# A merged latent entry, queries projected early, a later copy, and unread products on TensorE in the last batch and behind it

## The chip, the cores and the metric

One core of a Trainium2 chip runs the whole program in one launch. The metric is the device time in microseconds (us), the median of repeated runs. Five engines work side by side: PE (TensorE, matrix products), DVE (VectorE), ACT (ScalarE), POOL (GpSimd, which also issues the indirect DMAs, the ones that take row numbers from a tile) and SP (SyncE, which issues plain DMAs). Each engine runs its own list of instructions in order and waits on semaphores. All data are float32.

## The reference, cut to what matters

```python
# B = 16 batches of T = 112 tokens, D = 256, context of S = 375 rows, 16 heads of 64
x = x + L0_xcond(layernorm(x), cond, ctx)     # block 0: self-attention, cross-attention, gated GELU feed-forward
x = x + L0_ffn(layernorm(x))                  # 64 experts, the best 8 of each token, and a shared one
x = x + L1_xcond(ctx, layernorm(x), cond)     # latent attention: keys from layernorm(ctx) and the latents
x = x + L1_ffn(x)                             # 8 experts, the best one of each token
# in L1_xcond: lat = layer_norm(layernorm(x)) * w + b, so that the rows are normalised twice
```

## The kernel before, in words

The program has four stages, one after the other. The order on each engine is written by hand. Only semaphores tie the engines together.

**Block 0** (16 batches, the function `batch(b, begin, last)` on every engine; batches 1 to 14 are a hardware loop). PE does for a batch: scores, transposes and outputs of the self-attention; `project_out(wo1)`; values of the context; a transpose of the normalised rows (`transpose_h(hn2)`); the first half of the cross queries (`wq2`, heads 0 to 7); a transpose of the *next* batch's rows (`transpose_h(hn1)`); then `attention`, the cross-attention, in four steps k = 0, 2, 4, 6 of two head pairs each. Within a step PE makes scores (L966), DVE their negated maxima (`nmax`, L2126), ACT the exponentials (`probs`, L1678), PE transposes them (L978), DVE and ACT copy the transposes (`probsT`), and PE multiplies with the values (L991). The hook `late` puts work between the scores and the transposes of step 0: the ranks of the routing of the batch before, and the second half of the cross queries, into the PSUM bank `psO[:, 1]`. Behind the attention follow the projections of the next batch's queries and keys (`half_qk(wq1)` twice, `half_qk(wk1)` twice), and then `project_out(wo2)`, which waits for DVE's scaled outputs `oT` (L2077). Last comes the feed-forward with its 64 instructions of up projection (`fw1`) and `project_out(fw2)`. ACT computes `hT1` and `hT2` from the transposed rows (`affine`, L1709). The same DVE does the routing of the batch before in small chained pieces (`slots`, with `route_piece` between the steps), and POOL scatters the routed slots to a table in memory, each scatter behind a numbered job of DVE (`SCATTER_JOBS`).

**Experts 0.** Behind the last batch come the shared expert's products (`shared_up`, `shared_down`), the counting of the routed rows (`tables0`), a gather of the row numbers (`idrow`), a transpose of them (L1316), and then `blocks0`, which takes 144 blocks of rows: POOL gathers their rows, PE transposes them (L1405), DVE copies the transposes (`xT0`, L2582), PE multiplies (L1421, L1433), and ACT stores the results to `ydram`, in memory as `expert_rows` (L1815).

**Latent attention** (16 batches, `batchL`). Its entry: keys and values of the first context; DVE adds the eight expert rows of each token to X (`add_rows`, L2661), which POOL has gathered into `yk` by `fetch0` (L795, eight indirect DMAs); statistics; `latents0` on DVE normalises the rows of batch 0 twice in a row, with two inverse roots (`inverse_root_column`, three Newton steps each); PE transposes the latents (L1572) and projects them. Then DVE adds the expert rows of batch 1, all eight in a row, before it takes up the first attention. POOL does for each later batch `latents(b)`, `fetch0(b + 1)` and `context_rows(b + 1)`. PE's `transpose_kv(b)` needs `lat_ready`, which POOL's `latents(b)` raises. `fetch0(0)` follows a wait for all stores of experts 0.

**Experts 1** is the last stage. Its first two weights, of 2 MB each, are issued by SP (`weights1(0)`, `weights1(1)`) as soon as the last product of experts 0 is done.

## Time and profile before

| what | value |
|---|---|
| median of 3 runs | 2773.25 us (2772.94 to 2776.93) |
| the profiled execution | 2777.12 us, its span 2775.0 us |
| PE busy | 2649.2 us, 95% of the span |
| DVE busy | 1515.7 us, 55% |
| ACT busy | 1101.0 us, 40% |
| POOL busy | 903.2 us, 33% |
| mean granted clock of TensorE | 0.984 |

The span runs from the first to the last instruction. A clock of 1.00 is TensorE's full speed (2.4 GHz), 0.50 is the other level (1.2 GHz). The ends of PE's instructions are modelled, so that an idle time before a matmul is good to about a tenth of a microsecond.

### The profile page before, as it was taken

Reading aid. Unit: us, or ns where it says so; the run is one execution under the profiler, and the core shown is the slowest. Engines: PE = TensorE matmul, PEld = TensorE weight load, DVE = VectorE, ACT = ScalarE, POOL = GpSimd, SP = SyncE. Lnnn points to the kernel's source line nnn. Section 1 sums busy time; section 2 is a strip of 40 time slices with the busy share of each in tenths; the row PEclk is TensorE's granted clock in tenths of the full one; section 3 lists DMA queues with packets and bytes.
Section 4 is the critical chain, followed back from the end, with each engine's and each line's share of the span. In section 5 each row is a group of like instructions: output and inputs, shape, how many; then the busy total and the mean of one; then the engine's idle time right before and its main releaser. Section 6 shows DMA issues by size and latency. Waiting matters only on the chain. (4 is left out here: it accounts for less than half of the span.)

```text
span 2775.0 us, 61020 instructions
## 1 busy us (share of the span) xinstructions
PE 2649.2 (95%) x18023; PEld 1838.3 (66%) x18024; DVE 1515.7 (55%) x4435; ACT 1101.0 (40%) x2902; POOL 903.2 (33%) x1743
## 2 busy tenths in 40 slices
PE   8999999999999999998899988999999999999698
PEld 5777776777777767775566645665666665656597
DVE  4555555555555555555666645655556655554332
ACT  2443444334434443343366623443334433334222
POOL 2121112222211222221455526444444344440343
PEclk9999999999999999999899999999999999999799
DMA  7000000000000000002588841000010000100351
GB/s 243 4 9 7 9 9 9 9 9 3 7 7 9 9 9 9 9 4 99 173 255 254 198 127 38 26 22 22 22 39 27 22 22 22 30 18 5 99 179 26
DMA packets 87780, 145.65 MB, mean 52 GB/s; under 512 B 22418, under 2 KB 64399, under 8 KB 86176
## 3 DMA queue, kind: packets, MB, share of 16 engines
q1 hardware_dynamic: 44320, 84.85, 9.6%
q0 software_dynamic: 20848, 41.09, 5.7%
q10 hardware_dynamic: 22544, 18.89, 2.0%
q8 instruction: 33, 0.54, 0.1%
q14 instruction: 35, 0.29, 0.0%
HBM read 116.17 MB, written 29.51 MB: 53 GB/s over the span
## 5 line engine op out<-in xcount | busy, mean ns | idle before, releaser
L1037 PE MATMUL psG<-W,ctxT 128*125 128x512 f32 (+2 forms) x896 | 406.8, 597 | 4.8 <-DVE v L2754 4.8
L1031 PE MATMUL psG<-ctxT,W 128*128 128x375 f32 (+1 forms) x1024 | 385.6, 524 | 2.8 <-ACT ctxT L1910 1.5
L1031 PEld LDWEIGHTS psG<-ctxT,W 128*128 128x128 f32 x1024 | 189.3, 190 | 161.3 <-issue 106.7
L1678 ACT ACTIVATE probs<-psG,nmax 112x375 f32<-112x375 f32 (+1 forms) x384 | 233.1, 618 | 147.2 <-DVE nmax L2126 147.2
L1037 PEld LDWEIGHTS psG<-W,ctxT 128*125 128x125 f32 (+2 forms) x896 | 160.8, 187 | 180.6 <-issue 170.2
L1025 PEld LDWEIGHTS psG<-hT,W 128*128 128x128 f32 x2304 | 267.3, 194 | 17.1 <-ACT hT L1709 14.8
L1025 PE MATMUL psG<-hT,W 128*128 128x112 f32 x2304 | 272.2, 278 | 1.9 <-ACT hT L1709 1.9
L2126 DVE TENSOR_REDUCE nmax<-psG 112x1 f32<-112x375 f32 (+1 forms) x384 | 208.6, 599 | 64.3 <-PE psG L966 60.2
L664 POOL DMA_INDIRECT slot_table<-stt,st x120 | 114.1, 951 | 340.7 <-DVE qT L2155 124.3
L991 PEld LDWEIGHTS psO<-probsT,v 125*64 125x64 f32 (+2 forms) x3584 | 173.3, 137 | 65.2 <-issue 61.1
L991 PE MATMUL psO<-probsT,v 125*64 125x112 f32 (+2 forms) x3584 | 200.5, 263 | 0.0
L966 PE MATMUL psG<-kT,qT 64*112 64x375 f32 (+1 forms) x768 | 169.6, 545 | 19.1 <-ACT hT L1709 17.8
L771 POOL DMA_INDIRECT W<-normed_rows,ids x144 | 136.2, 946 | 127.8 <-PE psG L1405 101.1
L1049 PE MATMUL psG<-W,oT 128*112 128x256 f32 x768 | 173.9, 380 | 2.0 <-DVE oT L2077 2.0
L1049 PEld LDWEIGHTS psG<-W,oT 128*112 128x112 f32 x768 | 133.5, 177 | 36.0 <-issue 9.8
L978 PE MATMUL psG<-ident,probs 112*122 112x112 f32 (+1 forms) x1120 | 143.8, 267 | 2.9
L1421 PE MATMUL psG<-W 128*64 (+1 forms) x936 | 141.6, 390 | 0.2
L795 POOL DMA_INDIRECT mlp<-expert_rows,st x128 | 121.0, 945 | 47.5 <-issue 35.2
L1942 ACT ACTIVATE v<-psG 122x512 f32<-122x512 f32 x64 | 38.2, 597 | 242.6 <-PE psG L1037 242.6
L978 PEld LDWEIGHTS psG<-ident,probs 112*122 112x122 f32 (+1 forms) x1120 | 110.6, 140 | 25.3 <-ACT probs L1678 16.1
L2754 DVE COPY v<-psG 122x512 f32<-122x512 f32 x64 | 44.2, 691 | 131.9 <-PE psG L1037 131.9
L966 PEld LDWEIGHTS psG<-kT,qT 64*112 64x112 f32 x768 | 62.0, 173 | 67.7 <-ACT hT L1709 20.9
(428 smaller groups left out, 4704.3 us busy)
## 6 DMA issues: line engine op xcount, KB each, us to landing
W<-in_ew SPq DMA_DIRECT2D x64, 384.0 KB, 4.3
expert_rows<-W ACTq DMA_DIRECT2D x144, 128.0 KB
W<-in_ew SPq DMA_DIRECT2D x8, 2048.0 KB, 8.3
ctxT<-in_ctxT SPq DMA_DIRECT2D x16, 375.0 KB, 3.1
kT<-in_ctx SPq DMA_DIRECT2D x16, 375.0 KB
normed_rows<-hrow SPq DMA_DIRECT2D x32, 112.0 KB, 1.9
W<-normed_rows,ids POOLq DMA_INDIRECT x144
slot_table<-stt,st POOLq DMA_INDIRECT x136, 2.1
```

The source lines that it names most:

```text
L771: nc.gpsimd.indirect_dma_start(out=xg0[:, j % 4, :], out_offset=None, in_=hd, in_offset=bass.IndirectOffsetOnAxis(ap=ids[:, j:j + 1], axis ...
L795: nc.gpsimd.indirect_dma_start(out=yk[:, k, :], out_offset=None, in_=ydram[0], in_offset=bass.IndirectOffsetOnAxis(ap=st8[:, 0, k:k + 1], ...
L966: nc.tensor.matmul(pair_bank(order, slot, i)[0:T, 0:keys], qT[DH * i:DH * i + DH, u, :], kT[DH * i:DH * i + DH, u, 0:keys], start=True, st ...
L978: mm = nc.tensor.transpose(pair_bank(order, turned_slot(u), i)[0:ke, c * T:(c + 1) * T], probs[:, 2 * (u % 2) + i, k0:k0 + ke], ident[0:T, ...
L991: mm = nc.tensor.matmul(psO[DH * i:DH * i + DH, u // 4, (u % 4) * T:(u % 4 + 1) * T], v[0:kn, c, h * DH:(h + 1) * DH], probsT[0:kn, u % 2, ...
L1025: mm = nc.tensor.matmul(bank[:, j * T:(j + 1) * T], wt[:, c, n0 + j * P:n0 + (j + 1) * P], hT[:, c, :], start=(c == 0), stop=(c == DC - 1))
L1031: mm = nc.tensor.matmul(bank[:, 0:n], wt[:, c, n0 + j * P:n0 + (j + 1) * P], src[:, c, 0:n], start=(c == 0), stop=(c == DC - 1))
L1037: mm = nc.tensor.matmul(bank[0:kn, 0:512], src[:, c, k0:k0 + kn], wt[:, c, n0 + half * 512:n0 + (half + 1) * 512], start=(c == 0), stop=(c ...
L1049: mm = nc.tensor.matmul(bank[0:T, 0:D], oT_[:, c, :], wo[:, c, :], start=(c == 0), stop=(c == n - 1))
L1421: mm = nc.tensor.matmul(psG[half * h:half * h + half, 2 + j.m2, 0:256], xT0[:, j.m, c, half * h:half * h + half], weights(c, k, h), start= ...
L1678: nc.scalar.activation(probs[:, 2 * (u % 2) + i, 0:keys], pair_bank(order, scores_slot(u), i)[0:T, 0:keys], ACT.Exp, bias=nmax[:, h:h + 1] ...
L2126: nc.vector.tensor_reduce(nmax[:, 2 * u + i:2 * u + i + 1], pair_bank(order, scores_slot(u), i)[0:T, 0:keys], AXX, ALU.max, negate=True).t ...
```

## The change

Six edits:

- *Early queries.* In batches 0 to 14 PE projects the second half of the cross queries ahead of the attention's scores, not between scores and transposes. At that old place it now projects the first half of the next batch's keys (`next_keys`, bank `psO[:, 0]`), so that one projection less stands behind the attention. DVE copies these keys there; ACT copies the second half. DVE's routing pieces move back by one, the last three to a new place `behind` the attention, and POOL's scatters change the jobs that they wait for.
- *Later copy.* In the self-attention DVE normalises two tiles of `probs` before it copies the first transpose (`self_copy(0)`).
- *Unread products.* `keep_busy` multiplies the identity with a piece of W; nobody reads the result. Five such products of 512 columns stand ahead of the last batch's second `transpose_h(hn2)`, one ahead of its `project_out(fw2)`, four ahead of the transpose of the row numbers, and two of 256 columns each behind the transposes of blocks 0, 1 and 2.
- *One root for two norms.* `latents` and `latents0` compute one inverse root with a folded constant in place of two in a chain.
- *Merged entry.* DVE copies values between its additions, and adds the rows of batch 1 in two fours around the copy of the keys. On POOL `entry` takes the gathers of batch 2 in pairs between the context rows and the latents of batch 1.
- *Later weights.* SP issues the first two weights of experts 1 behind its loop over the latent batches.

```diff
+EPS_TWICE, GAIN_TWICE = EPS * EPS / (1.0 + EPS), 64.0 * (1.0 + EPS)
-        SCATTER_JOBS = (0, 8, 9, 11, 12, 13, 14, 15)
+        SCATTER_JOBS = (0, 9, 10, 11, 12, 13, 14, 15)
...
             experts0(L0E, S0)
-            sp.wait_ge(S0.y_full, L0E.NBLK + 1)
-            weights1(0)
-            weights1(1)
...
                 context_of(b)
                 store_rows1(b - 3)
+            sp.wait_ge(S0.y_full, L0E.NBLK + 1)
+            weights1(0)
+            weights1(1)
...
+            def entry():
+
+                fetch0(1, True)
+                fetch_slots(2, True)
+                context_rows(1, between=fetch_some)
+                latents(1, fetch_some)
+                context_rows(2)
...
+            def keep_busy(out, n):
+
+                for _ in range(n):
+                    nc.tensor.matmul(out, ident[:], W[:, 20992:20992 + 512][:, 0:out.shape[-1]], start=True, stop=True)
...
+            def next_keys():
+
+                pe.wait_ge(act_evac, act.now())
+                dve.next()
+                project_T(wk1, hT1, 0, 4, psO[:, 0, :]).then_inc(dve_full, 1)
+                return {0: (dve_evac, dve.now())}
...
-                pe.wait_ge(act_evac, q2_done)
-                banks = held(1, 1) if not last else held(0, 1)
+                if last:
+                    pe.wait_ge(act_evac, q2_done)
+                    banks = held(0, 1)
+                    second = None
+                else:
+                    a, d = act.now(), dve.now()
+                    banks = {act.turn: (act_evac, a), 2 + dve.turn: (dve_evac, d)}
+                    second = late_queries()
+                    pe.wait_ge(act_evac, a - 1)
+                    pe.wait_ge(dve_evac, d - 1)
...
                 if not last:
-                    for side in range(2):
-                        half_qk(wk1, "k1", side)
+                    project_T(wk1, hT1, 512, 4, bank_for_act()).then_inc(act_full, 1)
                 pe.wait_ge(w_in["o2"], 16)
                 project_out(wo2, oT, IC)
...
+                if last:
+                    keep_busy(psO[:, 0, :], 5)
                 pe.wait_ge(hn2_ready, 2 * b + 2)
                 transpose_h(hn2)
...
+                if last:
+                    keep_busy(psO[:, 0, :], 1)
...
                 shared_down(2)
+                keep_busy(psG[:, 0, :], 4)
                 pe.wait_ge(s.idrow_ok, 1)
...
                             mm.then_inc(s.xT_full, 1)
+                            if lo == 0 or (lo == 1 and k == i):
+                                keep_busy(psG[:, 3, 256:512], 2)
...
+            def queries_and_keys(r, last):
+
+                if r is not None:
+                    places(r)
                 late_queries()
+                if r is not None:
+                    slots(r, 0)
+                if not last:
+                    next_keys()
...
-                self_copy(0)
                 self_normalise(2)
                 self_normalise(3)
+                self_copy(0)
```

The next piece is PE's program in the loop of block 0, from the first half of the cross queries (`psG<-hT,W`) over the transpose of the next batch's rows (`norms`) to the first transposes of `probs`. Before:

```order
87 L1025 MATMUL psG<-hT,W 128x112 x8
88 L1192 REGISTER_ALU
89 L1055 MATMUL psG<-ident,norms 128x112 x2
90 L1194 REGISTER_ALU
91 L965 REGISTER_ALU
92 L966 MATMUL psG<-kT,qT 112x375 x4
93 L1134 MATMUL psT<-cumr,ones 112x64
94 L1135 MATMUL psT<-mskr,before 112x64
95 L1025 MATMUL psO<-hT,W 128x112 x8
96 L975 ISA
97 L978 MATMUL psT<-ident,probs 126x112 x3
```

And of the change:

```order
88 L1046 MATMUL psG<-hT,W 128x112 x8
89 L1220 REGISTER_ALU
90 L1081 MATMUL psG<-ident,norms 128x112 x2
91 L1046 MATMUL psO<-hT,W 128x112 x8
92 L1230 REGISTER_ALU
93 L986 REGISTER_ALU
94 L987 MATMUL psG<-kT,qT 112x375 x4
95 L1160 MATMUL psT<-cumr,ones 112x64
96 L1161 MATMUL psT<-mskr,before 112x64
97 L1046 MATMUL psO<-hT,W 128x112 x8
98 L996 ISA
99 L999 MATMUL psT<-ident,probs 126x112 x3
```

A second projection of 8 products now stands ahead of the scores (row 91), and the one behind them (row 97) is that of the keys.

DVE's program at the entry of the latent attention, from the first copy of values (L2754) to the first key copy of the latents (L2157); `X<-mlp,wgt,X` is `add_rows`, `R` is the latent tile. Before:

```order
665 L2661 SCALAR_TENSOR_TENSOR X<-mlp,wgt,X 112x256 x4
666 L2754 COPY v<-psG 122x512
667 L2661 SCALAR_TENSOR_TENSOR X<-mlp,wgt,X 112x256 x4
668 L2677 BN_STATS cst<-X 112x6
...
690 L2741 TENSOR_SCALAR R<-X,cmv,ry 112x256
691 L2754 COPY v<-psG 122x512 x2
692 L2730 TENSOR_SCALAR ctxT<-psG,affL 128x112
693 L2155 TENSOR_SCALAR qT<-psG 128x448
694 L2157 COPY kT<-psG 128x4x112
695 L2754 COPY v<-psG 121x512
696 L2661 SCALAR_TENSOR_TENSOR X<-mlp,wgt,X 112x256 x8
```

And of the change:

```order
665 L2813 COPY v<-psG 122x512
666 L2722 SCALAR_TENSOR_TENSOR X<-mlp,wgt,X 112x256 x4
667 L2813 COPY v<-psG 122x512
668 L2722 SCALAR_TENSOR_TENSOR X<-mlp,wgt,X 112x256 x4
...
681 L2800 TENSOR_SCALAR R<-X,cmv,ry 112x256
682 L2791 TENSOR_SCALAR ctxT<-psG,affL 128x112
683 L2213 TENSOR_SCALAR qT<-psG 128x448
684 L2722 SCALAR_TENSOR_TENSOR X<-mlp,wgt,X 112x256 x4
685 L2215 COPY kT<-psG 128x4x112
686 L2722 SCALAR_TENSOR_TENSOR X<-mlp,wgt,X 112x256 x4
687 L2813 COPY v<-psG 121x512
```

Between the statistics (row 668) and the latents (`R`) stood 21 rows and now stand 10. POOL's program from the end of the context's root to the latents of batch 1, in the change:

```order
178 L284 TENSOR_TENSOR cry<-cry,crt 128x3
179 L799 DMA mlp<-expert_rows,st 112x256 x2
180 L650 TENSOR_SCALAR v<-kT,cmv,cry 125x256
181 L799 DMA mlp<-expert_rows,st 112x256 x2
182 L650 TENSOR_SCALAR v<-kT,cmv,cry 125x256
183 L799 DMA mlp<-expert_rows,st 112x256 x2
184 L650 TENSOR_SCALAR v<-kT,cmv,cry 125x256
185 L814 TENSOR_TENSOR R<-X,cmv 112x256
186 L799 DMA mlp<-expert_rows,st 112x256 x2
```

Before, the three context rows stood in one piece, the latents with their two roots behind them, and the eight gathers behind the latents.

## Rows read from the trace of the kernel before

**Rows 1.** One window behind the last batch: length; busy us of each engine (instructions), PEclk, DMA share, GB/s.

```profile
1336.00:1352.00 16.00, 11.24 (x39) 6.72 (x40) 9.20 (x38) 1.65 (x4) 7.79 (x9) 0.50 0.24 69
```

**Rows 2.** Waits of PE in the whole span: us in total, times, longest.

```profile
PE psG L966 <- ACT hT L1709: 17.8, 15, 1.3
...
PE psT L934 <- DVE probs L2095: 3.0, 14, 0.6
```

**Rows 3.** Timeline of one loop batch, ahead of the cross-attention: start, duration.

```profile
460.77 1.94 PE L1025 MATMUL psG<-hT,W 128*128 128x112 f32 x16
...
462.54 0.36 PE L1055 MATMUL psG<-ident,norms 112*128 112x112 f32 x2
...
464.08 1.52 PE L966 MATMUL psG<-kT,qT 64*112 64x375 f32 x8 [1.18 <-ACT hT L1709]
```

**Rows 4.** Timeline of the same batch, step 2 of the cross-attention.

```profile
471.79 1.64 PE L978 MATMUL psG<-ident,probs 112*126 112x112 f32 x12
...
472.20 0.58 ACT L1678 ACTIVATE probs<-psT,nmax 112x375 f32<-112x375 f32 x1
```

**Rows 5.** Timeline of another loop batch, behind the cross-attention.

```profile
406.75 5.52 PE L1025 MATMUL psG<-hT,W 128*128 128x112 f32 x48
407.23 1.16 DVE L2077 TENSOR_TENSOR oT<-psO,mlp 128x448 f32<-128x448 f32 x2 [3.69 <-ACT mlp L1649]
```

**Rows 6.** Timeline of PE, up projections of a loop batch.

```profile
423.04 7.37 PE L1025 MATMUL psG<-hT,W 128*128 128x112 f32 x64
```

**Rows 7.** Timeline of PE in the last batch and behind it.

```profile
1284.44 0.63 PE L1055 MATMUL psG<-ident,hn 112*128 112x112 f32 x2 [4.59 <-DVE hn L2007]
1286.00 9.71 PE L1025 MATMUL psG<-hT,W 128*128 128x112 f32 x64 [0.93 <-ACT hT L1709]
...
1336.66 0.47 PE L1316 MATMUL psT<-ident,W 128*128 128x128 f32 x1 [4.72 <-DVE W L2473]
1336.93 3.62 PE L1263 MATMUL psO<-W,mlp 128*112 128x256 f32 x8
...
1346.24 1.12 PE L1405 MATMUL psG<-ident,W 128*128 128x128 f32 x4 [2.59 <-DVE W L2582]
```

**Rows 8.** DMA issues from 1610 to 1630: size in KB, us to landing.

```profile
W<-in_ew SPq DMA_DIRECT2D x2, 2048.0 KB, 11.1
```

**Rows 9.** Timeline at the entry of the latent attention.

```profile
1612.89 0.34 SPq L519 DMA_DIRECT2D W<-in_ew  x1
...
1624.15 0.96 POOL L795 DMA_INDIRECT mlp<-expert_rows,st  x1 [0.80 <-POOL st L792]
...
1625.10 8.74 PE L1037 MATMUL psG<-W,ctxT 128*122 128x512 f32 x20
...
1635.70 2.25 DVE L2661 SCALAR_TENSOR_TENSOR X<-mlp,wgt,X 112x256 f32<-112x256 f32 x4 [8.19 <-DMA mlp<-expert_rows,st]
...
1644.75 0.21 DVE L288 TENSOR_SCALAR ve<-ry 112x1 f32<-112x1 f32 x2
...
1648.23 0.45 PE L1572 MATMUL psG<-ident,R 112*128 112x112 f32 x1 [6.24 <-DVE R L2741]
...
1664.27 4.59 DVE L2661 SCALAR_TENSOR_TENSOR X<-mlp,wgt,X 112x256 f32<-112x256 f32 x8
...
1672.44 1.75 PE L978 MATMUL psT<-ident,probs 112*122 112x112 f32 x8 [6.97 <-ACT probs L1678]
```

**Rows 10.** Timeline of POOL from the context's root of batch 1, and PE.

```profile
1671.22 0.26 POOL L277 TENSOR_SCALAR cve<-cmv 128x3 f32<-128x3 f32 x1 [19.47 <-DVE cmv L2264]
...
1676.11 3.65 POOL L648 TENSOR_SCALAR v<-kT,cmv,cry 125x256 f32<-125x256 f32 x3 [0.18 <-POOL cry L283]
...
1689.78 0.61 POOL L811 TENSOR_TENSOR R<-R,ry 112x256 f32<-112x256 f32 x1
1694.20 0.48 PE L1512 MATMUL psG<-ident,v 125*128 125x125 f32 x3
```

**Rows 11.** Groups of the whole span: busy us, mean ns; idle before.

```profile
L795 POOL DMA_INDIRECT mlp<-expert_rows,st x128 | 121.0, 945 | 47.5 <-issue 35.2
```

114 lines of the change are left out of this document (63 added, 51 removed).

## The prediction

> **What bounds the kernel now.** I read the windows of 50 us first, over the whole span, for the busy time of TensorE and its granted clock. PE is busy for 95% of the span, so a gain has to be a stall of PE that goes, or PE work that runs at the full clock and not at half. The list of PE's waits then names the stalls. Two of them come back in every batch of block 0: the scores of the cross-attention wait for ACT's rows of the next batch, 17.8 us in 15 times, and the transposes of the self-attention wait for DVE, 3.0 us in 14 [rows 2]. The timelines of the two passages behind block 0 show the rest: waits of 4.6 and 4.7 us, and work at half the clock behind each [rows 1, 7]. At the entry of the latent attention PE waits 6.2 us for the latents and 7.0 us for the first exponentials [rows 9]. The rest of PE's time is work that the change neither adds nor takes away.
>
> **Block 0, early queries.** In the row of a loop batch the first projection starts at 460.77, the transposes at 462.54, the scores at 464.08, after 1.18 us of idle time [rows 3]. By starts, a projection of 16 instructions costs 1.77 us; behind the attention three take 5.52, 1.8 each; 64 instructions in 7.37 agree [rows 5, 6]. The transposes cost 0.2. In the changed order the second query projection runs in the wait: 460.77 + 1.77 + 0.2 + 1.8 = 464.54, so that the scores start 0.46 us later than now. By then ACT's rows are long there. Between scores and transposes stands one projection before and after, so this stretch keeps its length. Behind the attention there is one projection less, 1.8 us. Net 1.8 - 0.46 = 1.34 us for each of the 15 batches, 20.1 us. By the idle column alone it would be 17.8, and nothing if a new wait takes the place: these are the bounds of the term.
>
> Two new waits have to be looked at. (1) `project_out(wo2)` is reached 1.8 us earlier. The three projections start at 406.75, two of them end at about 410.4, and `oT` is complete at 407.23 + 1.16 = 408.4 [rows 5]. That leaves 2.0 us. The routing pieces that now stand ahead of the `oT` products fall into the 3.69 us for which DVE waits there for ACT, and are three operations on 8 columns. Priced at nothing; without this cover each microsecond of them would cost 15 in all. (2) DVE now has to copy the keys, 448 columns, before it copies the first transposes, with one routing piece less ahead of it. Behind these copies are queued the maxima of step 2, for them waits ACT, for ACT's exponentials PE. In step 2 the fourth exponential ends at 472.20 + 0.58 = 472.78, and PE takes it up with the last quarter of its transposes, at 471.79 + 1.23 = 473.0 [rows 4]. So the slack is 0.2 us. I reckon DVE 0.2 to 0.4 us late there, because the piece that goes is shorter than the copy that comes; 0.2 us a batch past the slack over 14 batches is -2.8 us. The later self-attention copy takes away the second recurrent wait: +3.0 at most, and it costs nothing, since the copy is needed only after two more transposes; I take 2.7. Block 0: 20.1 - 2.8 + 2.7 = 20.0 us.
>
> **The last batch and behind it, unread products.** A product of 512 columns is two instructions; 20 of these take 8.74 us [rows 9], 0.87 us a product. Five are 4.35 us in a wait of 4.59, four are 3.5 us in one of 4.72 [rows 7], and the single one stands where PE waits for DVE's last gated half. So none delays what follows, as long as the clock is full. Today the 64 instructions behind the first wait take 9.71 us, against 7.37 in a loop batch [rows 6, 7]: the granted clock had fallen to the lower level after PE stood still. With PE busy up to 0.2 us before the transposes they should run at the full clock: 9.71 - 7.37 = 2.3, and 0.3 for the transposes, 2.6 us. All that follows hangs on this chain (gelu, down projection, routing of the last tile, tables), so it passes through.
>
> Behind the second wait (from 1336) the clock is 0.50 for 16 us, in which PE is busy 11.2 us [rows 1]. At the full clock this work is 5.6 us shorter, if all of it were on the path. It isn't: two gathers and DVE's copies set the pace in part. The eight shared products of 3.62 us end 1.8 us earlier, and DVE's queue (sum, row numbers, slots, first copy of a block) with them, so the transposes of block 2 start about 1.8 us earlier than 1346.24 [rows 7]. Of the work behind them some 2 us more shrink, less 0.87 for two unread products that stand between the transposes of blocks 2 and 3. I take 3.0 us; the bounds are 0 and 5.6. Together 5.6 us.
>
> **The latent entry.** The gathers of batch 0's expert rows start at 1624.15, because POOL first waits for the last stores of the experts to memory. In this same stretch the two weights of 2 MB are on their way: issued from 1612.89 on [rows 9], when the last product is done, they land 11.1 us later [rows 8], just when POOL starts; the stores share the DMA engines with them. With the weights moved to the end of the latent stage, where the core's DMA engines are nearly idle, I let the first gather start at 1617, 7 us earlier. Eight gathers at 0.945 us and 0.31 us between them [rows 11] take 10.0 us and the last lands 2.8 us after its issue (1624.15 + 8.8 + 2.8 = 1635.7, as the row has it), so the rows are there at 1628.6. From then on PE's values set DVE's pace: half a value costs 1.72 us from 1625.10 on (four instructions of 0.43), so VectorE's halves are ready at 1628.5, 1632.0 and 1635.4. Between them DVE adds four rows in 2.25 us each time: the additions end at 1635.1 and not at about 1640.8. Statistics 0.8, the last copy 0.7, one root 2.7 and the normalised rows 0.4: the latents are there at 1639.8. Today PE gets them at 1648.23. One root less is 3.1 us of that (the second starts at 1644.75) [rows 9].
>
> The next link is batch 1's expert rows. POOL gathers them behind the additions of batch 0: 1635.1 + 1.3 + 8.8 + 2.8 = 1648.0. DVE adds four (to 1650.3), copies the keys, adds four (1653.5), copies the last values when PE has them (1654.9), measures (0.8 and 1.5) and takes up the first maxima at 1657.2. The exponentials come 1.5 us behind: PE's transposes start at about 1658.7, against 1672.44 now [rows 9]: 13.7 us. PE's own queue isn't the limit there: the projections, values and scores end near 1655.5, even with some 2 us at half clock.
>
> The price is on POOL. Its run from the context statistics to the latents of batch 1 is now 1671.22 to 1690.4, 19.2 us, of which the latents with two roots are 10.6 (from 1676.11 + 3.65) and one root 5.2 [rows 10]. In the changed order it is 19.2 - 5.2 + 8 x 1.25 = 24.0 us from 1657.2, so to 1681.2. PE reaches the transposes that need it 21.8 us after its first ones (1694.20 - 1672.44) [rows 9, 10]: 1658.7 + 21.8 = 1680.5. A new wait of 0.7 us, where there were 3.8 us of slack. The entry: 13.7 - 0.7 = 13.0 us.
>
> **The rest.** Weights 0 and 1 are needed one stage later and have about two batches of the latent loop to land; the DMA engines are nearly idle there. In the steady latent loop POOL gets shorter, but nobody waits for it. Both at nothing. Sum: 20.0 + 5.6 + 13.0 = 38.6 us. Against the profiled execution 2777.1 - 38.6 = 2738.5; this one stands 3.9 above the median of 2773.25, so the median should be 2734.7.
>
> **A rule against it.** The eight gathers of batch 2 now run while DVE copies transposes in the first attention. In the page's row a gather costs 945 ns in the mean over 128 of them, whatever DVE does beside it, and most of these 128 stand beside DVE's copies [rows 11]. The Trainium skill (SBUF — State Buffer, on the "DVE blocks DMA" trap) says that a DMA issued by GpSimd needs a port that a VectorE copy in a two-port mode holds for its whole length, so that a transfer of some 620 ns took some 3100 beside such a copy. By it the run on POOL would grow by several microseconds, which is the third rival below; the trace speaks for the row.
>
> **Rivals.** *A. DVE becomes the bound in step 2* of the cross-attention: the whole copy of 0.62 us stands on the path and not 0.2. For it: the slack of 0.2 [rows 4]. Against: the copy falls where DVE would wait for the first transposes. 14 batches at 0.6 to 0.7 us more: 9 us, 2744. *B. The clock isn't held*: the second stretch stays at 0.50, and the unread products then cost twice their time ahead of the row numbers (7 us in a wait of 4.7, 2.3 on the path). The first 2.6 stay, the 3.0 go and 2.3 are added: 2740. *C. The entry gives less*: the stores weren't held up by the weights (fetch at 1624 as now, then 13.0 becomes about 9), or POOL's mixed run takes 5 us more because a gather stands for a copy: 2739 to 2743. *D. No change*: the wait for ACT moves to another instruction, and the entry's gain is eaten by POOL; 2768 to 2778. *E. Slower*: the mechanism of A in every step of the attention, since the maxima, once late, keep ACT and PE late. It decides from 38.6 / 15 = 2.6 us a batch, or 0.65 us in each of four steps; at 0.8 a step it ends at 2783. Against it: DVE has idle time ahead of the maxima in each later step, and less routing in the last.
>
> **How the numbers follow.** My case 57%, with a range of its own from 2728 to 2742 (block 0 between 15 and 23 us, behind it 3 to 8, entry 10 to 15). A 14%, B 9%, C 13%, D 3%, E 4%. The likeliest is 2735. Without D and E, and with the lower end of the clock and entry bounds, 8 of 10 lie between 2727 and 2749. 0.2% is 5.5 us and is about what a measurement can tell from no change here: faster 93%, within 3%, slower 4%.
>
> **What would show it.** Right: L966's wait for `hT` is gone from PE's list, the batch of block 0 is 1.3 to 1.5 us shorter, and no new wait over 0.2 us stands at `project_out(wo2)` or at the transposes of step 2; the clock is 1.00 from 1280 to 1292 and behind the row numbers; the 64 instructions take 7.4 us; the first gather of the latent entry starts under 5 us after the last expert product; PE's first transposes there come some 14 us earlier, with a small wait at the next transposes of the context. Wrong: PE waits for `probs` in each batch (A, E), 0.50 in the windows behind the last batch (B), POOL's run over 26 us (C). The prediction as a whole fails if block 0 gives less than 10 us.

## The result and the profile after

The changed kernel takes 2733.41 us (median of 4 runs, 2726.93 to 2734.23), against 2773.66 for the kernel before beside it (4 runs, 2772.94 to 2776.93). The ratio is 0.9848, with a 95% interval of 0.983 to 0.9865: 40.2 us faster, where 2735.0 was forecast. The profiled execution of the changed kernel took 2733.2 us, its span 2731.2, which is 43.8 below the span of before. The two differences are 3.6 us apart, because the profiled execution of before stood 3.5 us above its median (2777.12 against 2773.66) and that of the changed kernel did not.

The line of busy time from the page of the changed kernel:

```profile
PE 2648.2 (97%) x18055; PEld 1841.4 (67%) x18056; DVE 1517.4 (56%) x4423; ACT 1102.6 (40%) x2902; POOL 853.4 (31%) x1548
```

PE does the same 2648 us of work, now in 97% of the span: what went is idle time. PE's waits over the whole span (us in total, times, longest) say which:

```profile
PE psT L999 <- ACT probs L1728: 8.3, 13, 2.3
...
PE psG L1622 <- DVE R L2800: 4.0, 1, 4.0
...
PE psG L987 <- ACT qT L1753: 0.7, 1, 0.7
```

The two recurrent waits of [rows 2] are gone, and no other took their place: the 8.3 us are 13 waits, all in the latent stage. The wait for the latents (6.24 in [rows 9]) is 4.0, the one for the row numbers (4.72 in [rows 7]) is 2.2. A new wait of 1.1 us for POOL, which the prediction put at 0.7, stands in the timeline of the entry below; the 0.7 us for `qT` is in the last batch, whose queries stand where they stood, and it is as long in the kernel before.

Timeline of one loop batch of the changed kernel on PE, from the self-attention to `project_out(wo2)` (L1070; L955 are the self-attention's transposes, L966 its outputs, L1046 projections, L987 scores, L1160 the ranks):

```profile
436.16 1.89 PE L1058 MATMUL psG<-W,ctxT 128*125 128x512 f32 x4
437.89 0.95 PE L955 MATMUL psT<-ident,probs 112*112 112x112 f32 x8
438.79 1.77 PE L966 MATMUL psO<-probsT,v 112*64 112x112 f32 x32
...
451.67 1.94 PE L1046 MATMUL psG<-hT,W 128*128 128x112 f32 x16
...
453.64 1.95 PE L1046 MATMUL psO<-hT,W 128*128 128x112 f32 x16
455.52 1.52 PE L987 MATMUL psG<-kT,qT 64*112 64x375 f32 x8
...
477.35 3.74 PE L1046 MATMUL psG<-hT,W 128*128 128x112 f32 x32
480.92 3.62 PE L1070 MATMUL psG<-W,oT 128*112 128x256 f32 x16
```

The end of the same stretch in the kernel before, behind the first projection of 460.77 in [rows 3]:

```profile
485.91 5.52 PE L1025 MATMUL psG<-hT,W 128*128 128x112 f32 x48
491.27 3.62 PE L1049 MATMUL psG<-W,oT 128*112 128x256 f32 x16
```

The second query projection starts where PE stood still in [rows 3], the scores 3.85 us behind the first projection (3.31 before), and behind the attention two projections take 3.57 by starts where three took 5.36. From 451.67 to 480.92 are 29.25 us; the same two starts of before are 30.50 apart.

Since each batch has the same places, the starts of PE's rows can be set against each other stage by stage. The table holds differences of starts, in us; its first column counts from the start of the span. The places are: `project_out(wo2)` of batch 0; the same of the last batch; its down projection; the transposes of blocks 6 and 7 of the experts (the expectations below call this place block 4, but the four instructions at 1325.09, 1355.12 in the kernel before, belong to 6 and 7); the transposes of the first latent context (1612.79 before); POOL's first gather of expert rows, counted from there; the transposes of the next context that need POOL's latents of batch 1 ([rows 10]); the end of the span. The kernels below "changed" are the experiments.

| kernel | to `wo2` of batch 0 | to that of the last | to down projection | to block 6 | to latent context | (first gather) | to batch 1's latents | to the end |
|---|---|---|---|---|---|---|---|---|
| before | 95.77 | 1180.39 | 20.75 | 58.21 | 257.67 | 11.36 | 81.41 | 1080.8 |
| changed | 94.10 | 1155.66 | 18.22 | 57.11 | 257.49 | 3.60 | 68.55 | 1080.1 |
| copy_back | 95.74 | 1163.23 | 18.22 | 56.39 | 259.66 | 3.61 | 67.55 | 1080.0 |
| queries_back | 96.41 | 1173.21 | 18.22 | 58.09 | 258.76 | 3.59 | 68.54 | 1080.6 |
| weights_back | 95.42 | 1155.59 | 18.22 | 56.08 | 257.01 | 11.29 | 74.55 | 1081.5 |
| no_block_products | 94.14 | 1155.62 | 18.22 | 58.06 | 258.09 | 3.60 | 67.31 | 1081.1 |
| no_products | 95.04 | 1156.09 | 20.74 | 58.13 | 257.58 | 3.60 | 68.68 | 1080.4 |
| six_products | 94.52 | 1155.68 | 18.22 | 56.48 | 257.81 | 3.60 | 68.51 | 1080.3 |
| pool_apart | 95.47 | 1155.70 | 18.22 | 55.96 | 258.94 | 3.60 | 67.88 | 1078.7 |
| roots_back | 95.36 | 1156.14 | 18.23 | 55.64 | 259.03 | 3.61 | 77.74 | 1081.7 |
| hold | 94.88 | 1156.16 | 18.22 | 57.72 | 266.35 | 3.60 | 69.17 | 1080.4 |
| apart_six | 94.61 | 1155.71 | 18.22 | 56.50 | 265.98 | 3.60 | 75.69 | 1079.1 |
| dve_late | 95.35 | 1156.84 | 18.22 | 57.63 | 266.15 | 3.61 | 69.13 | 1080.6 |
| copy_alone | 96.03 | 1173.09 | 19.98 | 58.11 | 265.40 | 12.02 | 82.06 | 1096.8 |

The last four ran on another chip than those above; the kernel before took 2803.04 us there, and has no trace from that chip. The gain of 43.8 us of span is 1.7 + 24.7 + 2.5 + 1.1 + 0.2 + 12.9 + 0.7. Of the 1.7 us in the first column, 1.3 are batch 0's early queries (from its first cross projection to its `wo2` are 30.19 us before and 28.85 changed) and the rest is the start-up, which differs by up to 1.4 us between kernels that are alike there (94.10 to 95.47). Block 0 thus gained 26.1 us. A loop batch, from one `wo2` to the next, takes 77.40 us (median), and 79.17 before.

Behind the last batch PE now reads (L1076 are unread products; the clock is 1.00 in each window from 1250 to 1270):

```profile
1253.27 4.46 PE L1076 MATMUL psO<-W,ident 128*128 128x512 f32 x10
...
1259.38 7.40 PE L1046 MATMUL psG<-hT,W 128*128 128x112 f32 x64 [0.93 <-ACT hT L1759]
...
1267.98 3.68 PE L1070 MATMUL psG<-W,mlp 128*112 128x256 f32 x16 [0.32 <-issue]
```

Five products lie in the wait of [rows 7], and the 64 instructions take 7.40 us, not 9.71. The second stretch went otherwise; windows and PE's timeline of the changed kernel:

```profile
1306.00:1308.00 2.00, 0.57 (x3) 0.53 (x4) 0.85 (x4) 0.00 (x0) 1.32 (x2) 1.00 0.14 43
...
1310.00:1312.00 2.00, 0.63 (x2) 0.18 (x1) 1.33 (x6) 0.00 (x0) 1.39 (x3) 0.50 0.21 66
...
1318.00:1320.00 2.00, 2.00 (x13) 1.46 (x14) 0.85 (x2) 0.00 (x0) 1.15 (x2) 0.84 0.15 49
```

```profile
1307.43 0.33 PE L1364 MATMUL psT<-ident,W 128*128 128x128 f32 x1 [2.19 <-DVE W L2534]
1307.60 2.82 PE L1310 MATMUL psO<-W,mlp 128*112 128x256 f32 x8
...
1312.73 1.92 PE L1076 MATMUL psG<-W,ident 128*128 128x256 f32 x4
...
1315.76 1.92 PE L1076 MATMUL psG<-W,ident 128*128 128x256 f32 x4
```

The clock was at the lower level from about 1308.4 to 1318.6, where it had been there for 16 us [rows 1]. PE had paused for 2.19 us before the row numbers. The shared products took 2.82 us (3.62 in [rows 7]), and each pair of unread products behind a block 1.92 us and not 0.87.

The entry of the latent attention in the changed kernel, POOL, PE and DVE by time (L799 gathers, L2722 additions of expert rows, L819 the end of POOL's latents of batch 1):

```profile
1586.18 0.96 POOL L799 DMA_INDIRECT mlp<-expert_rows,st  x1 [0.80 <-POOL st L794]
...
1609.32 0.63 PE L1622 MATMUL psG<-ident,R 112*128 112x112 f32 x2 [3.97 <-DVE R L2800]
1617.64 2.25 DVE L2722 SCALAR_TENSOR_TENSOR X<-mlp,wgt,X 112x256 f32<-112x256 f32 x4 [0.25 <-DMA mlp<-expert_rows,st]
...
1626.67 0.26 POOL L278 TENSOR_SCALAR cve<-cmv 128x3 f32<-128x3 f32 x1 [3.23 <-DVE cmv L2325]
...
1627.87 1.25 PE L999 MATMUL psT<-ident,probs 112*122 112x112 f32 x8 [2.27 <-ACT probs L1728]
...
1632.17 1.02 POOL L799 DMA_INDIRECT mlp<-expert_rows,st  x1 [0.79 <-POOL cry L284]
...
1650.46 0.61 POOL L819 TENSOR_TENSOR R<-R,ry 112x256 f32<-112x256 f32 x1
1651.13 0.54 PE L1562 MATMUL psG<-ident,v 125*128 125x125 f32 x3 [1.14 <-POOL R L819]
```

Counted from PE's transposes of the first latent context at 1582.58, the gather comes after 3.60 us (11.36 before), the latents after 26.7 (35.4), the first transposes of the exponentials after 45.3 (59.65), and those that need batch 1's latents after 68.6 (81.4). POOL's run from the context statistics to these latents is 24.4 us; 24.0 was forecast.

### The profile page after: what moved, and what is told of

It is laid out like the page before. It is cut to its first block, busy times and chain, and to the rows that moved or that the text cites. A ratio compares the mean times of both kernels' runs of the same rounds, so it can differ in the third digit from the quotient of the medians.

```text
span 2731.2 us, 60580 instructions
## 1 busy us (share of the span) xinstructions
PE 2648.2 (97%) x18055; PEld 1841.4 (67%) x18056; DVE 1517.4 (56%) x4423; ACT 1102.6 (40%) x2902; POOL 853.4 (31%) x1548
## 4 chain that ended last, share of the span: by engine, by line
PE 86%; ACT 5%; DVE 3%; issue 3%; POOL 1%; DMA 1%; DVEq 0%; ACTq 0%; POOLq 0%; SPq 0%
PE psG L1058 16%; PE psG L1052 14%; PE psG L1046 11%; PE psG L1070 8%; PE psG L1471 5%; PE psO L1012 5%; ACT probs L1728 4%; PE psG L987 4%; PE psG L999 3%; PE psG L1537 3%; PE psO L1548 3%; PE psO L1483 2%; PE psO L1046 2%; PE psT L999 2%; PE psT L987 2%
## 5 line engine op out<-in xcount | busy, mean ns | idle before, releaser
L1058 PE MATMUL psG<-W,ctxT 128*125 128x512 f32 (+2 forms) x896 | 405.1, 595 | 0.0
L1058 PEld LDWEIGHTS psG<-W,ctxT 128*125 128x125 f32 (+2 forms) x896 | 160.7, 186 | 175.1 <-issue 170.5
L1046 PEld LDWEIGHTS psG<-hT,W 128*128 128x128 f32 x2064 | 238.4, 193 | 16.9 <-ACT hT L1759 14.7
L2176 DVE TENSOR_REDUCE nmax<-psG 112x1 f32<-112x375 f32 (+1 forms) x384 | 208.6, 599 | 70.6 <-PE psG L987 64.8
L1046 PE MATMUL psG<-hT,W 128*128 128x112 f32 x2064 | 243.3, 277 | 1.9 <-ACT hT L1759 1.9
L1070 PE MATMUL psG<-W,oT 128*112 128x256 f32 x768 | 173.9, 380 | 2.0 <-DVE oT L2127 2.0
L987 PE MATMUL psG<-kT,qT 64*112 64x375 f32 (+1 forms) x768 | 170.0, 547 | 1.3 <-ACT qT L1753 0.7
L1070 PEld LDWEIGHTS psG<-W,oT 128*112 128x112 f32 x768 | 133.5, 177 | 35.9 <-issue 9.8
L799 POOL DMA_INDIRECT mlp<-expert_rows,st x128 | 121.1, 946 | 47.0 <-issue 34.5
L1471 PEld LDWEIGHTS psG<-W 128*64 128x64 f32 x936 | 75.0, 136 | 43.7 <-issue 12.9
```

The costliest lines, as they stand in the source:

```text
L799: nc.gpsimd.indirect_dma_start(out=yk[:, k, :], out_offset=None, in_=ydram[0], in_offset=bass.IndirectOffsetOnAxis(ap=st8[:, 0, k:k + 1], ...
L987: nc.tensor.matmul(pair_bank(order, slot, i)[0:T, 0:keys], qT[DH * i:DH * i + DH, u, :], kT[DH * i:DH * i + DH, u, 0:keys], start=True, st ...
L1046: mm = nc.tensor.matmul(bank[:, j * T:(j + 1) * T], wt[:, c, n0 + j * P:n0 + (j + 1) * P], hT[:, c, :], start=(c == 0), stop=(c == DC - 1))
L1058: mm = nc.tensor.matmul(bank[0:kn, 0:512], src[:, c, k0:k0 + kn], wt[:, c, n0 + half * 512:n0 + (half + 1) * 512], start=(c == 0), stop=(c ...
L1070: mm = nc.tensor.matmul(bank[0:T, 0:D], oT_[:, c, :], wo[:, c, :], start=(c == 0), stop=(c == n - 1))
L1471: mm = nc.tensor.matmul(psG[half * h:half * h + half, 2 + j.m2, 0:256], xT0[:, j.m, c, half * h:half * h + half], weights(c, k, h), start= ...
```

## The experiments

**copy_back.** The old place of one copy, all else as changed.

```diff
                 self_invert(1)
+                self_copy(0)
                 self_normalise(2)
                 self_normalise(3)
-                self_copy(0)
```

> The changed kernel, with DVE's first self-attention copy ahead of the two normalisations again. Theory of the prediction: the old order costs what PE's idle column named, 0.2 us a batch, so the span grows from 2731.2 by 2.7 to 2734. Rival: it costs the whole length by which the stretch from the first transposes of the self-attention to the outputs shrank (444.74 to 447.88, now 436.16 to 438.79: 3.14 against 2.63 us), 0.5 us a batch, since the end of PE's transposes and their weight loads also wait there; the span grows by 7.7 to 2739.

Measured: 2742.79 us (2742.19 to 2743.29) beside 2776.41 for before, ratio 0.9877 (0.9861 to 0.9894), span 2740.8. From `wo2` to `wo2` it grew by 7.57 us, a loop batch from 77.40 to 77.93 us. PE in its self-attention:

```profile
439.77 1.89 PE L1058 MATMUL psG<-W,ctxT 128*125 128x512 f32 x4
441.84 1.13 PE L955 MATMUL psT<-ident,probs 112*112 112x112 f32 x8 [0.18 <-DVE probs L2145]
442.90 1.78 PE L966 MATMUL psO<-probsT,v 112*64 112x112 f32 x32
```

From the value projection (L1058) to the outputs are 3.13 us, against 2.63 above. The idle column names 0.18 us of the 0.5. The rest hides in the row itself: the eight transposes have a length of 1.13 us and not 0.95, and their start is 0.34 us later behind the projection. The rival was right, and the prediction's reading of the idle column wrong.

**queries_back.** The old order of queries and keys on PE, ACT, DVE and POOL; the later copy stays.

```diff
-                    second = late_queries()
...
-                    return second, next_keys()
...
-                    project_T(wk1, hT1, 512, 4, bank_for_act()).then_inc(act_full, 1)
+                    for side in range(2):
+                        half_qk(wk1, "k1", side)
```

> The changed kernel, with the old order of the queries and keys in block 0 (PE, ACT, DVE's routing pieces, POOL's scatter places); the later copy and all else stay. Theory 1, two independent parts: the queries are worth 1.25 us a batch (first cross projection to project_out(wo2) 30.50 before, 29.25 after), 18.8 us in all, span 2750. Theory 2, the parts are tied: the self-attention is late only because something in the old order holds DVE, and the copy alone gives 2.7; then the span grows by 26.5 - 2.7 = 23.8 to 2755. The lateness of 0.2 us in step 2 that I priced would show as less than 18.8, near 16.

Measured: 2755.15 us (2752.24 to 2756.71), ratio 0.992 (0.9903 to 0.9936), span 2753.8. From `wo2` to `wo2` it grew by 17.55 us, a loop batch from 77.40 to 78.66, 1.26 us, and batch 0 by 1.36, 18.9 in all. PE's wait for `hT` was back with 17.8 us in 15 times. Theory 1 holds: the parts are independent (7.6 + 18.9 = 26.5, the whole is 26.1). The rest of the 22.6 us of span lies in the start-up (1.0) and in the stretches behind block 0.

**weights_back.** The two weights of experts 1 at their old place in SP's program.

```diff
             experts0(L0E, S0)
+            sp.wait_ge(S0.y_full, L0E.NBLK + 1)
+            weights1(0)
+            weights1(1)
```

> The changed kernel, with the first two weights of experts 1 issued at the old place, behind the last product of experts 0. Theory: they share the DMA engines with the last stores, so the first gather of the latent entry comes 7 to 8 us later (from 1586.2 to about 1594) and the whole entry with it: span +7 to +8, 2739. Rival 1 (C of the prediction): the stores take this long anyway and the fetch came earlier for another reason, so the first gather stays at 1586 and the span at 2731. Rival 2: the gather is late, but half of it is hidden behind the values of the first context: +4.

Measured: 2740.66 us (2739.95 to 2742.57), ratio 0.9872 (0.9855 to 0.9888), span 2738.4. The first gather came 11.29 us behind the context transposes, as in before (11.36), against 3.60. So 7.7 of the 7.8 us by which it came earlier are due to the weights. The latents came 5.5 us later and batch 1's 6.0; PE's wait for `R` was 9.5 us and not 4.0.

Of 7.7 us, 1.7 to 2.2 are absorbed by DVE's copies and PE's values in between. Rival C of the prediction, whose ground was that the stores take this long by themselves, is out.

**no_block_products, no_products, six_products, hold.** In order: without the products behind blocks 0 to 2; without any; six ahead of the row numbers; six, and five more of 256 columns behind them.

```diff
-                            if lo == 0 or (lo == 1 and k == i):
-                                keep_busy(psG[:, 3, 256:512], 2)
```

> The changed kernel without the unread products behind the transposes of blocks 0, 1 and 2; those in the last batch and ahead of the row numbers stay. Theory 1, they cost: at half the clock each pair takes 1.9 us in PE's queue, and without them the transposes of block 2 start 1.8 us earlier and the span is 1 to 2 us shorter. Theory 2, they pay: the clock comes back at 1318.3 because PE is busy from 1312.7 on; without them it stays at 0.50 until about 1322, the up products of blocks 0 and 1 take 3.7 and 1.9 instead of 1.95 and 1.5, and the span is 1 to 2 us longer. Both together: within 0.5 us.

> The changed kernel without any unread product. Theory: the first group (five and one) is worth 2.5 us, all between the last wo2 projection and the down projection of the last batch (20.75 us before, 18.22 with them): this stretch should read 20.7 again. The second group is worth about 1 us between the down projection and the transposes of block 4 (58.2 before, 56.1 to 58.1 in four kernels with them): 58 to 58.5. Span against the changed kernel +3.5. Rival: the stretches got shorter by another part of the change, such as SP's later weights or what comes earlier from block 0; then the first stays at 18.2 and the span grows by under 1.

```diff
-                keep_busy(psG[:, 0, :], 4)
+                keep_busy(psG[:, 0, :], 6)
```

> The changed kernel with six products, not four, ahead of the transpose of the row numbers, so that PE works until 0.5 us before they come (the wait of 2.19 us less two times 0.87). Theory: the clock is still 1.00 behind them, the eight shared products take 1.9 and not 2.8 us, and the unread products behind blocks 0 to 2 take 0.9 each and not 1.9: down projection to block 4 at or below 56.1, span 1 to 2 us shorter. Rival 1: the clock isn't bound to this wait but falls behind the next one, for the gathers (1.6 us), and nothing is won: within 0.5 us. Rival 2: the row numbers land earlier than PE is through, and it costs up to 0.9.

```diff
                 nc.tensor.transpose(psT[:, 1, 208:208 + L0E.NBLK - P], idrowf0[0:L0E.NBLK - P, 1, :],
                                     ident[0:L0E.NBLK - P, 0:L0E.NBLK - P]).then_inc(s.idT_full, 1)
+                keep_busy(psG[:, 3, 256:512], 5)
```

> The kernel with six products ahead of the row numbers, and five more of 256 columns behind the transpose of the last row numbers, into the wait of 2.5 us for the first gathered rows that took their place. Theory 1, the clock is what this passage costs: it stays at 1.00 through, the unread products behind blocks 0 to 2 take 0.9 each and not 1.0, 1.9 and 1.7, and down projection to block 4 falls from 56.5 to about 55. Theory 2, the gathers and DVE's slots are what it costs: the clock stays at 1.00, and block 4 still comes 56 to 57 behind the down projection, because PE waits for gathered rows instead; span within 0.7 us of the changed kernel.

Measured: 2735.43 us (ratio 0.9853, 0.9837 to 0.987), 2739.6 (0.9861, 0.9844 to 0.9877), 2733.31 (0.9837, 0.982 to 0.9853), and on the other chip 2744.9 (0.9788, 0.9775 to 0.9801). The first group of products is settled: without it the stretch to the down projection is 20.74 us, as before (20.75), in all kernels with it 18.22 or 18.23 (on the other chip copy_alone, which has no products either, reads 19.98), and the clock in no_products reads

```profile
1260.00:1262.00 2.00, 1.07 (x6) 1.02 (x6) 0.00 (x0) 0.78 (x2) 0.00 (x0) 0.50 0.99 413
1262.00:1264.00 2.00, 2.00 (x11) 2.00 (x11) 0.00 (x0) 0.00 (x0) 0.00 (x0) 0.50 0.57 218
```

The second group is smaller and noisier. From the down projection to block 6, the three kernels of the first chips that lack the block products take 58.06 to 58.21 us, and the seven that have them 55.64 to 58.09, 56.5 in the mean: 0 to 2.6 us, of which some is given back up to the latent context. Over both columns the three without read 315.7 to 316.2, and the seven with them 313.1 to 316.9, 314.9 in the mean: 1.0 us, with a scatter of 1.2 from kernel to kernel. no_block_products, which keeps the four, reads 316.2 and no_products 315.7: what the four alone bring is not more than the scatter. No run shows that the block products cost time, although they run at the lower clock; whether they bring 1 us isn't settled, since the gathers in this stretch land at another time in each kernel and the clock falls at another time too. In pool_apart, for instance, four products were enough to keep it up behind the row numbers:

```profile
1309.66 0.33 PE L1364 MATMUL psT<-ident,W 128*128 128x128 f32 x1 [1.82 <-DVE W L2534]
1309.83 1.89 PE L1310 MATMUL psO<-W,mlp 128*112 128x256 f32 x8
```

There the clock fell only at 1314.5, behind the wait for the gathers, for some 3 us, as in copy_back, weights_back, roots_back and six_products: these five take 55.6 to 56.5 us to block 6. The other five of the first chips, with 7 to 17 us at the lower level, take 57.1 to 58.2. Over both columns the two groups are 314.6 and 315.8 in the mean. With six products the clock was 1.00 behind the row numbers, down to 1315.3, and the shared products took 1.89 us, but the wait for the gathers grew:

```profile
1308.08 0.33 PE L1364 MATMUL psT<-ident,W 128*128 128x128 f32 x1 [0.77 <-DVE W L2534]
1308.24 1.89 PE L1310 MATMUL psO<-W,mlp 128*112 128x256 f32 x8
...
1312.85 0.44 PE L1453 MATMUL psG<-ident,W 128*128 128x128 f32 x2 [2.54 <-DMA W<-normed_rows,ids]
```

In hold the clock did not fall in this passage (windows, then PE's timeline):

```profile
1308.00:1310.00 2.00, 2.00 (x6) 0.90 (x5) 1.24 (x5) 0.00 (x0) 0.14 (x1) 1.00 0.14 51
...
1316.00:1318.00 2.00, 1.43 (x7) 0.85 (x6) 1.34 (x7) 0.00 (x0) 1.65 (x2) 1.00 0.41 119
```

```profile
1315.09 1.03 PE L1076 MATMUL psG<-W,ident 128*128 128x256 f32 x4
1316.30 0.44 PE L1454 MATMUL psG<-ident,W 128*128 128x128 f32 x2 [0.17 <-DMA W<-normed_rows,ids]
...
1318.18 0.44 PE L1454 MATMUL psG<-ident,W 128*128 128x128 f32 x2 [0.58 <-DVE W L2644]
...
1322.53 0.66 PE L1454 MATMUL psG<-ident,W 128*128 128x128 f32 x4 [0.94 <-DVE W L2644]
```

The unread products take half as long, and PE waits for a gather (0.17) and for DVE's copies (0.58, 0.94) instead: 57.7 us. Its neighbour dve_late, same chip and only the four products there, is no comparison at the lower level: its row numbers came after 0.54 us, its clock was 1.00 throughout too, and it took 57.63. The comparison is apart_six, same chip, at 0.50 from 1313.0 to 1316.4: it took 56.50. So on this chip a clock held at 1.00 wins nothing here, which is theory 2 of hold: the gathers and DVE set the pace of this passage. On the first chips the short stretches at the lower level go with 1 to 2 us less up to block 6, and no run there held the clock throughout, so that how much of this the clock itself is worth stays open.

**roots_back.** Two chained roots on both engines again.

```diff
-                r = ry[0:T, 2:3]
+                var, r1, r2, left = cmv[0:T, 3, 1:2], ry[0:T, 3:4], ry[0:T, 1:2], ry[0:T, 0:1]
...
+                inverse_root_column(nc.gpsimd, note, chain, r2, left, rt[0:T, 0:1], ve[0:T, 0:3])
```

> The changed kernel with two inverse roots in a chain again, in DVE's latents of batch 0 and in POOL's of the others. Theory (the prediction's terms): the latents of batch 0 come 3.1 us later, and all behind them; POOL's run to the latents of batch 1 is 5.2 us longer than 24.4, and PE's wait for it goes from 1.1 to 6.3: span +8.3, 2739.5, and nothing in the steady loop. Rival: DVE's second root lies beside PE's values and POOL's is hidden for all but 1 us, so that one norm for two is worth 3 us or less: 2734.

Measured: 2745.41 us (2744.56 to 2747.27), ratio 0.988 (0.9864 to 0.9897), span 2743.8. Batch 0's latents came 3.4 us later, PE's wait for POOL was 6.34 us, and batch 1's latents were 9.2 us later. Both terms were right (3.1 forecast for the first; the wait grew by the 5.2 of the second), and nothing hides them.

**pool_apart and apart_six.** POOL's entry in the old order, alone and with six products.

```diff
                 fetch0(1, True)
-                fetch_slots(2, True)
-                context_rows(1, between=fetch_some)
-                latents(1, fetch_some)
+                context_rows(1)
+                latents(1)
+                fetch0(2, True)
                 context_rows(2)
```

> The changed kernel, with POOL's entry in the old order: context rows 1, latents 1, then the eight gathers of batch 2, then context rows 2. Theory: the gathers between the rows make latents 1 late by 10 us, of which 1.1 show as PE's wait; apart, latents 1 are there at 1641 and not 1651, this wait is gone, and the gathers of batch 2 (1642 to 1652, landed at 1655) are still ahead of DVE's additions at 1659: span 1.1 us shorter. Rival 1: the next wait, ACT's ctxT of 1.1 us behind it, takes its place: 0. Rival 2: the merge was needed: DVE's additions of batch 2 wait for their rows, and the span grows by 1 to 3. If gathers beside DVE's copies were slow, those of this kernel, at another time of DVE's program, would differ from 0.94 us.

> The two edits that cost nothing so far taken together: POOL's entry in the old order (context rows 1 and latents 1 in one piece, then the gathers of batch 2), and six products ahead of the row numbers. Counted from the first output projection, the span was 2637.1 us for the changed kernel, 2635.4 for the first edit and 2637.0 for the second. If both are real they add up: 2635.3, 1.8 less than the changed kernel. If the 1.7 was scatter of the transfers, it is within 1 us of 2637.

Measured: pool_apart 2733.68 us (2731.66 to 2735.5), ratio 0.9838 (0.9822 to 0.9854), span 2730.9. PE's wait for POOL was gone and batch 1's latents came 0.7 us earlier; from batch 0's `wo2` on the span was 1.6 us shorter. Neither edit beats the changed kernel by more than the measurement tells. apart_six ran on the other chip and took 2748.71 us (ratio 0.9806, 0.9793 to 0.982), where hold took 2744.9. From context to batch 1's latents it needed 75.7 us, where hold needs 69.2. All engines by time, of this kernel:

```profile
1651.34 2.38 DVE L2176 TENSOR_REDUCE nmax<-psG 112x1 f32<-112x487 f32 x4 [0.76 <-PE psG L987]
...
1654.57 0.93 PE L999 MATMUL psG<-ident,probs 112*122 112x112 f32 x8
...
1658.49 0.93 POOL L799 DMA_INDIRECT mlp<-expert_rows,st  x1 [0.30 <-issue]
1661.23 0.62 DVE L2187 COPY probsT<-psT 122x448 f32<-122x448 f32 x1 [7.51 <-remote]
1661.29 0.54 ACT L1734 ACTIVATE probsT<-psT 122x448 f32<-122x448 f32 x1 [6.55 <-remote]
```

DVE and ACT stood still for 7.5 and 6.6 us behind finished transposes, until POOL's run of eight gathers was through. On the first chips the same run (1643.55 to 1653.25 in pool_apart) stopped nobody.

**dve_late.** The routing pieces divided as before, so that the key copy is added and nothing goes.

```diff
                     slots(r, 0)
+                    slots(r, 1)
...
-                for i in (((), (1,)), ((2, 3), (4, 5)), ((6,), (7, 8)), ((), ()), ((9, 10, 12), ()))[k][behind]:
+                for i in (((), (2,)), ((3, 4), (5, 6)), ((7,), (8, 9)), ((), ()), ((10, 12), ()))[k][behind]:
```

> The changed kernel, with DVE's routing pieces divided as before (two ahead of the key copy, one and two behind it and so on), so that in step 0 the copy of the keys is added to DVE's old work and nothing goes. Theory of the prediction: ACT's fourth exponential of step 2 has a slack of 0.2 us, and DVE is 0.4 late: the batch of 77.41 us grows by 0.2, span +2.8. Rival: the slack is larger, since the copy of the queries fills a gap in DVE's chain of routing instructions and the maxima wait for PE anyway (0.29 us in the changed kernel): the batch stays at 77.4, span +0. A third case, the lateness passes to every step: +0.4 or more a batch, +6.

Measured: 2743.02 us (2742.29 to 2745.95), ratio 0.9786 (0.9771 to 0.98). A loop batch is 77.46 us, against 77.43 in hold on the same chip; the last batch is 0.4 us longer. The rival is right: even with the whole copy added, next to nothing arrives late. DVE's rows of step 0 in the changed kernel show one reason:

```profile
456.44 1.91 DVE L2176 TENSOR_REDUCE nmax<-psG 112x1 f32<-112x375 f32 x4 [1.99 <-PE psG L987]
458.26 0.21 DVE L2276 TENSOR_TENSOR slotr<-psT,basef 112x64 f32<-112x64 f32 x1
458.39 0.62 DVE L2200 TENSOR_SCALAR qT<-psO 128x448 f32<-128x448 f32 x1
```

The copy of the queries (L2200) starts 0.13 us behind the first routing instruction; in the old order a chained instruction stood there and started 0.32 behind it. The independent copy fills the chain's gap. The other: DVE waits 0.29 us for PE ahead of the maxima of step 2.

**copy_alone.** The kernel before, with the later copy alone.

```diff
-                self_copy(0)
                 self_normalise(2)
                 self_normalise(3)
+                self_copy(0)
```

> The kernel before, with the later self-attention copy as its only change. Theory: its worth doesn't hang on the early queries; a batch of block 0 shrinks from 79.17 to 78.65 us (0.52, as the changed kernel lost when the copy went back), 7.3 us over block 0. Rival 1, the idle column of before is all there is: 0.2 a batch, 2.7. Rival 2: in the old order the 0.5 us goes into the later wait for ACT's rows, 1.18 us grows to 1.7, and nothing is won.

Measured, on the other chip: 2794.35 us (2790.5 to 2795.75) beside 2803.04, ratio 0.9968 (0.9955 to 0.9981), 8.7 us faster. From `wo2` to `wo2` are 1173.09 us where the kernel before had 1180.39 on the first chip, 7.30 less, and a loop batch 78.65 us: as the theory had it to the hundredth. Both rivals are out. The gain of the whole on this chip can't be split further, since the kernel before has no trace from it. The latent stage of copy_alone shows the same standstill as apart_six, in the order of before:

```profile
1692.23 0.54 ACT L1684 ACTIVATE probsT<-psG 122x448 f32<-122x448 f32 x1 [0.22 <-PE psG L978]
1701.60 0.54 ACT L1649 ACTIVATE mlp<-psT 128x448 f32<-128x448 f32 x1 [8.82 <-remote]
```

ACT waits 8.82 us behind its last copy, during POOL's eight gathers (1690.80 to 1700.51), and the stage from batch 1's latents on takes 1096.8 us, where every other row of the table has 1079 to 1082. Against the kernel before on the first chip, 9.5 of the 16 us stand ahead of the next output projection, and each of the ten batches from the third on takes 59.6 to 59.7 us and not 58.8; the last part is 3.6 us shorter.

## Why the prediction came out, point by point

- *Block 0, 20.0 us forecast, 26.1 measured,* outside the range of 15 to 23 given for it; a loop batch became 1.77 us shorter, where 1.3 to 1.5 had been named as the sign of being right. The mechanism of the early queries and the place of the later copy were right; two terms of the sum were mis-sized. The later copy was entered with 2.7, "+3.0 at most", from the idle column. It is worth 7.3 us (copy_alone) to 7.6 (copy_back). Second, the -2.8 for a late step 2 doesn't exist: dve_late adds all of the copy and costs 0.03 us a batch. The early queries were entered with 1.34 a batch, 20.1; queries_back shows 1.36 in batch 0, 1.26 in each loop batch and nothing in the last, 18.9. The margin at `project_out(wo2)`, priced at nothing, held.
- *First unread products, 2.6 forecast, 2.5 measured* (no_products: 20.74 against 18.22). The mechanism was right too: the clock is 1.00 with them and 0.50 without.
- *Second unread products, 3.0 forecast, 1.1 measured in the first stretch and 1.0 as a mean over kernels.* The step that failed is that behind the row numbers the clock would be full and "the transposes of block 2 start about 1.8 us earlier": they start 49.5 us behind the down projection, 49.3 before. Four products left a pause of 2.2 us, the clock fell, as rival B had it; but B's cost on the path (2.3) didn't come either. Where the shared products did run at 1.00 (pool_apart, six_products), the 1.8 us were lost again in a longer wait for the first gather (2.5 us, against 0.63 before), and in hold, with 1.00 throughout, gathers and DVE's copies set the pace.
- *Entry, 13.0 forecast, 12.9 measured.* weights_back and roots_back confirm its two causes: 6.0 for the weights, 9.2 for the second root with both ends undone alone, together 15.2 and so more than the whole: undone at once they would overlap in part (argued; this was not run). DVE's new order of copies and additions was undone by no run, so that its share isn't known. The merged run on POOL gives 1.1 us back as a wait. The first gather was 7.8 us earlier (7 forecast), the first exponentials 14.4 (13.7), the new wait 1.1 (0.7).
- *The rest, 0:* 0.7 to the end of the span, 0.2 up to the latent context and 0.3 in the start-up, all within the scatter of their columns.
- *The rule against it.* The gathers beside DVE's copies took 0.93 to 1.02 us in the merged run (1632.17 and on), as [rows 11] had it. The trap that the Trainium skill tells of (SBUF — State Buffer, on "DVE blocks DMA") did not show in POOL's rows in the entry. Nearly all that DVE did beside these gathers reads PSUM (L2176, L2187), so that this case hardly puts it to the test.

The sum was 5 us short of the span's gain (+6.1 in block 0, -2.0 behind the last batch, the rest together +1.1): for the profiled execution 2738.5 was forecast, and it took 2733.2. The median came closer, 2734.7 against 2733.4, because the 3.9 us taken off for the height of before's profiled execution made up for most of it. That was right as arithmetic, and chance as far as the miss goes.

## What to carry to other kernels

The idle column was only a lower bound of what a late operand cost PE here: read the stall as the difference between starts of the row ahead of the operand and the row behind its user, against the same distance with the operand early (here 0.18 us in the column, 0.53 in the period). Before pricing a higher clock, ask which other engine would then set the pace; of two stretches at the lower level one gave back all of its 2.5 us (PE alone on the path), the other about 1 (gathers and copies on it). A large prefetch beside the last small transfers of a stage can delay whoever waits for these (7.7 us here), and issued later, where the engines of the transfers are nearly idle, it cost nothing that a column shows.

## What was not expected of the hardware

- The same program differs by chip: before took 2773.66 to 2778.34 us beside three sets of runs, and 2803.04 beside the fourth. There the experts' blocks took 265.4 to 266.4 us, against 257.0 to 259.7, and the scatters of the routing needed 4.7 us to land (median), against 2.1.
- On that chip ACT, DVE and PE stand still for 6.5 to 8.9 us beside an unbroken run of eight gathers (apart_six, copy_alone), and not where the gathers come in pairs between other work (hold, dve_late: 69.2 and 69.1 us to batch 1's latents, against 68.6 on the first chip). It is not the entry alone: beside the unbroken runs of the later batches DVE stands still for 6.5 to 6.7 us in hold, where it is 2.9 in the changed kernel on the first chip. Its copy of the queries at 1754.65 in hold comes 1.8 us behind the end of the run; these batches take 58.8 us on both chips all the same. So the merged entry, which costs 1.1 us of waiting on the first chips, is worth 6.5 us there up to batch 1's latents, and the changed kernel's lead should be larger: the two kernels nearest to it stand at 0.9788 and 0.9786, and the changed kernel itself was not run there. What the engines wait for isn't settled: the profile gives no releaser in the program. One guess, argued only, is that the engines' own instructions, which come in by DMA, queue behind the gathers; the Trainium skill (Runtime: NRT & Kernel Launch, on instruction fetch mechanics) says that each engine fetches its next block of instructions through a DMA queue while it executes the current one. The traces don't bear it out: apart_six has one such transfer in its run (16 KB at 1653.61, done after 0.89 us) and none from 1655 to 1662, and pool_apart, where nobody stopped, has one too. No run here tells the guess from other causes.
